# Phase 1's statistics two batches ahead, a difference moved from GpSimd to VectorE, and the first normalisation kept in memory for the second phase

## The chip, the cores and the metric

One core of a Trainium2 chip runs the kernel. The metric is the device time of one execution in microseconds. Five engines work side by side: TensorE (PE, with its weight loads PEld), VectorE (DVE), ScalarE (ACT), GpSimd (POOL) and SyncE (SP), which here issues nearly all DMAs.

## What is computed

The input x has 8 sequences of 512 tokens with 128 features. The block is a layer norm, a Mamba-like branch, a small branch of binary weights, and a sum. The reference, cut:

```python
xn = _layernorm(x)                              # (x - mean) / sqrt(var + eps)
# branch 1, on xn
normed = rmsnorm(xn, input_norm_w)
x_z, z = split(normed @ in_proj_W)              # 256 channels each
xc = silu(conv4(x_z) + conv_b)
dt = clip(softplus(xc @ dt_W + dt_b), 0.001, 0.1)
Bp, Cp = xc @ B_W, xc @ C_W                     # 64 states
h = exp(dt * A) * h + dt * B * xc               # 512 steps, per channel and state
y = einsum(h, C) * silu(z)
x1 = xn + y @ out_proj_W
n2 = rmsnorm(x1, ffn_norm_w)
a = x1 + (silu(n2 @ gate_W) * (n2 @ up_W)) @ down_W
# branch 2, on xn: weights of +1 and -1 from booleans
b = s2 * (relu2(s1 * (relu2(s0 * ([xn, -xn] @ k0)) @ k1)) @ k2)
out = x + a + b
```

## The kernel before

**Phase 1** works through eight batches (a sequence each), the tokens over the 128 partitions, four to a partition. `batches` lays it out in slots: in slot s an engine runs, in an order written in its own `slot(at)`, the stages of several batches, `at(stage, d)` for batch s + d. On VectorE the order is: `moments` of batch s+1 (mean and variance of each token), rests of b of batch s-2, `dt_bias` s-1, `normalize` s+1, `b_to_sbuf` s-1, `exp_to_p` s-1 (two steps of a compensated log(1 + e^v)), second rests s-2, `dt_and_u` s-1. GpSimd: `norms` s+1 (from the variance to the factor of layer norm, `nrm[:, 1]`, and to the product of both norms' factors, `nrm[:, 5]`, by seven small instructions), `first_rest` s-2, `log_err` s-1 (the difference `soft[:, 2] - soft[:, 1]`), `second_rest` s-2. `normalize` writes the input of the in-projection, with both norms in one factor, so layer norm's result alone is nowhere kept. TensorE: transposition of the normalised batch s, `dt_products` and `bc_products` s-1, `project` s (projection and convolution in one, L682). ScalarE: parts of u, copies, exp and log of the softplus (a table load each), and last `silus` of batch s, which `dt_products` of the next slot wait for. After slot 0 (`prepare_scan`) VectorE and GpSimd clear large tiles for the scan. SP stores each batch's dt, u and b to memory (`store`), and loads batches 4 to 7 of x into the places of batches 0 to 3 once those are normalised.

**The scan** has 512 steps in 16 bodies of 32. Each step k: GpSimd multiplies half of the state by its decay (L623, two instructions), VectorE multiplies the other half in PSUM (L1259) and adds the first half's input (L1270, two), ScalarE computes the decays of two steps in one exponential of 2048 columns (L1041), two steps ahead, and copies the PSUM half to SBUF (L1061), TensorE adds the inputs (L773, L780) and contracts the state with C (L828). SP loads the decays' exponents (L422, two DMAs of 512 KB for two steps, six places) and the chunks of inputs (12 DMAs for 16 steps, L201 to L218).

**The finish** of a group of 32 tokens per sequence rides in the scan: the function `finish(g, k)` of each engine gives what it does at step k after the end of group g's own body (negative: in that body, so -7 is step 25). It normalises x anew: `K_STATS` -7 and `K_MOMENTS` -6 on VectorE, `K_RSTD_SUM` -5 and `K_RSTD` -4 on GpSimd (a power), `K_SHIFT` -2 on VectorE, `K_XN` 0 on ScalarE (two activations); then at 2 TensorE transposes xn, and so on through the output projection (9), gate, up and down products and the binary branch to the result at 38. SP's `load_tokens(g)` loads x for group g in the middle of body g, two DMAs of 64 KB.

The three things that set the order are these programs in order on each engine, semaphores between them, and SP's queue. Bodies 3 to 14 are a hardware loop of three bodies (four rounds).

Of the kernel before, what the change touches and what calls it, by code (L numbers as in the profile page):

```python
# [5 lines left out]
F32 = mybir.dt.float32  # L6
BF16 = mybir.dt.bfloat16
U8 = mybir.dt.uint8
ALU = mybir.AluOpType
# [7 lines left out]
def mamba_and_binary_mlp_block(nc: bass.Bass, x, norm_w, ffn_w, in_w, conv_w, conv_b, dt_w, dt_b, b_w, c_w,  # L17
# [54 lines left out]
    dt_stage = nc.dram_tensor("dt_stage", (2, T // TS, Q, TS, E), F32, kind="Internal").ap()  # L72
    b_stage = nc.dram_tensor("b_stage", (NP, HQ, HQ, 2, NS, T, 2 * N), BF16, kind="Internal").ap()

    with ExitStack() as ctx:
# [84 lines left out]
        b_parts = c1.enter_context(nc.sbuf_tensor("b_parts", [P, 2, NP, NJ, 2 * N], BF16))  # L160
        w_in = c1.enter_context(nc.sbuf_tensor("w_in", [P, 2 * E], F32))
# [67 lines left out]
        def load_chunk(sp, t, cb, hq):  # L229
# [9 lines left out]
                 "b_zeroed cb_placed u_hi_ready b_hi_ready u_r1_ready b_r1_ready u_mid_ready b_mid_ready w1_step")  # L239
# [35 lines left out]
        def pb(name, shape, dt=F32):  # L275
# [18 lines left out]
        f_stats = pb("f_stats", [P, GT, 6])  # L294
        f_mv = pb("f_mv", [P, GT, 2])
        f_nrm = pb("f_nrm", [P, 5, GT])
# [13 lines left out]
        names = ("f_x_loaded f_stats_ready f_mv_ready f_rstd_ready f_shift_ready f_xn_ready f_xn_t_ready f_xn_feat_ready "  # L310
# [3 lines left out]
                 "f_result f_stored f_rstd_sum f_mean_square f_rrms_sum")  # L314
# [6 lines left out]
        K_STATS, K_MOMENTS, K_RSTD_SUM, K_RSTD, K_SHIFT, K_XN, K_XN_T, K_XN_FEAT = -7, -6, -5, -4, -2, 0, 2, 3  # L321
# [84 lines left out]
        with nc.Block() as block:  # L406
            @block.sync
            def _(sp):
# [17 lines left out]

                def store(q, bb):
# [5 lines left out]
                                 ).then_inc(S[f"dt_stored{bb}"], 16)  # L433
                    u_rows, b_planes = u_stage[q % HQ, q // HQ, bb], b_stage[:, q % HQ, q // HQ, bb]
# [97 lines left out]
            def _(pool):  # L532
# [32 lines left out]

                def log_err(q, bb):
                    n = q * 2 + bb

                    if n == B - 1:
                        return  # L570
# [839 lines left out]
```

## Time and profile before

| | |
|---|---|
| median of 3 runs | 1098.99 us (1097.10 to 1102.58) |
| the profiled execution | 1097.32 us |
| its span, first to last instruction | 1095.5 us |
| mean granted TensorE clock | 0.964 of full speed |
| busy: PE, DVE, ACT, POOL | 956.2, 915.3, 922.9, 847.7 us |
| DMA | 333.74 MB, mean 305 GB/s |
| first step of the scan | 177.6 us |
| starts of scan bodies 4, 5, 6 | 399.7, 453.7, 513.4 us |

The page gives, for one profiled execution, each engine's busy time, forty slices of the span, the chain that ended last, and the costliest groups of instructions. The trace behind it can be asked for timelines, waits and windows. A body that ends in the loop's jump (453.7 to 513.4) is about 5 us longer than others.

### The profile page before, as it was taken

To read this page: it belongs to the slowest core of one execution; us is meant where nothing else is said; L and a number is where in the kernel's file an instruction comes from. 1 tells how busy PE (TensorE), PEld (TensorE's weight loads), DVE (VectorE), ACT (ScalarE), POOL (GpSimd) and SP (SyncE) were. 2 spreads that over 40 slices of the span, in tenths; PEclk is the share of its full clock that TensorE was granted. 3 is DMA by queue.
4 is the path that set the end of the run, shared out by engine and by line. 5 is a ranking of instruction groups with operands and counts; after the bars stand their busy time and mean duration, and the time that the engine had idled before them with its cause. 6 is when DMAs were issued, how large, how long until landed. Compare 5 with 4: busy or idle time off the path is not lost.

```text
span 1095.5 us, 28254 instructions
## 1 busy us (share of the span) xinstructions
PE 956.2 (87%) x8006; PEld 424.3 (39%) x8006; DVE 915.3 (84%) x2035; ACT 922.9 (84%) x1125; POOL 847.7 (77%) x1216
## 2 busy tenths in 40 slices
PE   5988883568999999997999997999999899999898
PEld 3565541113434343433433332433333334343436
DVE  5677673998989999997999997898998899998992
ACT  1656776899989999997999997899997999999981
POOL 6555523888888888886888887898887798988880
PEclk9999986999999999998999999999999899999999
DMA  5245359999999999997899999898989799989940
GB/s 156 102 163 183 145 215 358 353 345 354 343 349 334 347 355 354 358 348 309 337 357 352 347 348 343 296 346 345 367 323 371 260 363 355 363 334 373 374 150 11
DMA packets 81004, 333.74 MB, mean 305 GB/s; under 512 B 15152, under 2 KB 35504, under 8 KB 45488
## 3 DMA queue, kind: packets, MB, share of 16 engines
q1 hardware_dynamic: 80688, 331.11, 81.8%
q8 instruction: 73, 1.20, 0.4%
q14 instruction: 115, 0.94, 0.2%
q10 hardware_dynamic: 128, 0.49, 0.1%
HBM read 306.38 MB, written 25.17 MB: 303 GB/s over the span
## 4 chain that ended last, share of the span: by engine, by line
PE 34%; DVE 26%; POOL 20%; issue 14%; ACT 3%; DMA 1%; DVEq 1%; ACTq 0%; SPq 0%; POOLq 0%
POOL decayed L623 14%; PE ps L828 11%; DVE ps L1259 8%; PE ps L773 7%; DVE state L1270 6%; PE ps L913 6%; PE ps L927 4%; DVE h L1367 2%; DVE soft L1185 2%; POOL soft L573 1%; PE ps L891 1%; PE ps L899 1%; PE ps L696 1%; ACT state L1061 1%; DVE gated L1332 1%
## 5 line engine op out<-in xcount | busy, mean ns | idle before, releaser
L623 POOL TENSOR_TENSOR decayed<-decay,state 128x256 f32<-128x256 f32 x1024 | 725.4, 733 | 152.5 <-DVE state L1270 103.9
L1041 ACT ACTIVATE decay<-decay,a_col 128x2048 f32<-128x2048 f32 x256 | 514.0, 2008 | 26.2 <-issue 17.9
L1270 DVE TENSOR_TENSOR state<-decayed,ps 128x256 f32<-128x256 f32 x1024 | 407.5, 418 | 58.8 <-POOL decayed L623 41.2
L1259 DVE TENSOR_TENSOR ps<-decay,ps 128x512 f32<-128x512 f32 x512 | 352.8, 689 | 41.1 <-ACT state L1061 16.0
L828 PE MATMUL ps<-state,c_cols 128*32 128x256 f32 x4096 | 336.8, 402 | 0.0
L1061 ACT COPY state<-ps 128x512 f32<-128x512 f32 x512 | 287.8, 587 | 54.7 <-issue 37.4
L773 PE MATMUL ps<-moving,b_rows 64*128 64x256 bf16 x1024 | 204.0, 280 | 89.9 <-DVE ps L1259 86.6
L780 PE MATMUL ps<-moving,b_rows 64*128 64x256 bf16 x1024 | 205.1, 282 | 13.0 <-DMA b_rows<-b_stage 13.0
L913 PE MATMUL ps<-h,w 128*128 128x256 f32 x512 | 176.8, 432 | 0.8 <-DVE h L1367 0.8
L773 PEld LDWEIGHTS ps<-moving,b_rows 64*128 64x128 bf16 x1024 | 58.4, 95 | 262.9 <-DVE ps L1259 163.7
L828 PEld LDWEIGHTS ps<-state,c_cols 128*32 128x32 f32 x4096 | 82.1, 110 | 112.3 <-issue 103.2
L913 PEld LDWEIGHTS ps<-h,w 128*128 128x128 f32 x512 | 80.3, 193 | 93.0 <-issue 90.0
L780 PEld LDWEIGHTS ps<-moving,b_rows 64*128 64x128 bf16 x1024 | 57.6, 95 | 13.3 <-issue 13.2
L682 PE MATMUL ps<-n_feat,w_tap 128*128 128x512 f32 x128 | 58.0, 607 | 1.0 <-ACT n_feat L947 1.0
L927 PE MATMUL ps<-w,h 128*128 128x128 f32 x256 | 44.7, 299 | 0.3 <-ACT h L1101 0.3
L878 PE MATMUL ps<-xn_feat,w 128*128 128x256 f32 x128 | 44.2, 430 | 0.3 <-DVE result L1376 0.2
L709 PE MATMUL ps<-w_dt,xc_feat 128*128 128x256 f32 x128 | 32.8, 410 | 12.3 <-ACT xc_feat L957 12.3
L927 PEld LDWEIGHTS ps<-w,h 128*128 128x128 f32 x256 | 33.5, 192 | 24.2 <-issue 23.4
L709 PEld LDWEIGHTS ps<-w_dt,xc_feat 128*128 128x128 f32 x128 | 30.5, 328 | 14.7 <-ACT xc_feat L957 14.1
L682 PEld LDWEIGHTS ps<-n_feat,w_tap 128*128 128x128 f32 x128 | 24.4, 196 | 29.2 <-issue 29.2
L1185 DVE TENSOR_TENSOR soft<-soft 128x1024 f32<-128x1024 f32 x8 | 20.8, 2602 | 16.3 <-POOL soft L573 16.3
L1145 DVE TENSOR_SCALAR normed<-x_tok,mean_var,nrm 128x128 f32<-128x128 f32 x32 | 19.9, 754 | 15.6 <-POOL nrm L564 15.6
(124 smaller groups left out, 813.2 us busy)
## 6 DMA issues: line engine op xcount, KB each, us to landing
decay<-dt_stage SPq DMA_DIRECT2D x512, 512.0 KB, 6.3
moving<-u_stage SPq DMA_DIRECT2D x63, 256.0 KB
u_stage<-u_parts SPq DMA_DIRECT2D x16, 512.0 KB, 2.8
b_rows<-b_stage SPq DMA_DIRECT2D x63, 128.0 KB
b_stage<-b_parts SPq DMA_DIRECT2D x16, 384.0 KB, 3.3
dt_stage<-dt_tok SPq DMA_DIRECT2D x8, 512.0 KB, 3.1
moving<-u_stage SPq DMA_DIRECT2D x126, 32.0 KB
x_tok<-in_L_attn_x_dram SPq DMA_DIRECT2D x4, 512.0 KB, 4.0
```

Source lines behind the costliest of these rows:

```text
L623: nc.gpsimd.tensor_tensor(decayed[:, p], decay[:, dec_slot(m, k), p, k % TS, :], state[:, (k - 1) % RING, p * E:(p + 1) * E], ALU.mult).th ...
L682: m = nc.tensor.matmul(ps[:, XC + h, :], w_tap[:, k, h * P:(h + 1) * P], n_feat[:, bass.ds(n, 1), k:k + T].rearrange("d o t -> d (o t)"), ...
L709: m = nc.tensor.matmul(ps[:, DTT + j // 2, (j % 2) * E:(j % 2 + 1) * E], xc_feat[:, bb, h, j:T:NJ], w_dt[:, h, :], start=(h == 0), stop=(h ...
L773: return nc.tensor.matmul(ps[:, acc_bank(m, k), p * E:(p + 1) * E], b_rows[rows(1), cb, p, kk, :], moving[rows(1), cb, kk, :], start=False ...
L780: return nc.tensor.matmul(ps[:, SELFP + k % 2, p * E:(p + 1) * E], b_rows[rows(0), cb, p, kk, :], moving[rows(0), cb, kk, :], start=True, ...
L828: m = nc.tensor.matmul(ps[q * 32:(q + 1) * 32, YP, 0:E], c_cols[:, cb, q, kk * 2 * TC:(kk + 1) * 2 * TC], state[:, k % RING, q * E:(q + 1) ...
L913: m = nc.tensor.matmul(ps[:, FB, c * GTOK:(c + 1) * GTOK], w1[:, n, f:f + P], h1[:, n, :], start=(n == 0), stop=(n == H1 // P - 1))
L927: m = nc.tensor.matmul(ps[:, FB, j * P:(j + 1) * P], terms[c][0][:, j * P:(j + 1) * P], terms[c][1], start=(c == 0), stop=(c == len(terms) ...
L1041: nc.scalar.activation(pair, pair, ACT.Exp, scale=a_col[:, 2:3]).then_inc(decay_ready, 1)
L1061: nc.scalar.copy(state[:, k % RING, SELF:QE], ps[:, acc_bank(m, k), :]).then_inc(acc_copied, 1)
L1259: nc.vector.tensor_tensor(ps[:, acc_bank(m, k), :].rearrange("p (q e) -> p q e", q=HQ), decay[:, dec_slot(m, k), HQ:Q, k % TS, :], ps[:, a ...
L1270: nc.vector.tensor_tensor(state[:, k % RING, p * E:(p + 1) * E], decayed[:, p], ps[:, SELFP + k % 2, p * E:(p + 1) * E], ALU.add).then_inc ...
```

## The change

It does four things. VectorE's `moments` move from the head of slot s for batch s+1 to near its end for batch s+2 (batch 0 before all slots). The difference that GpSimd's `log_err` made is made by VectorE in `exp_to_p`, as it was for the last batch before. A new stage `xn_tokens` on VectorE writes layer norm's result of each batch (x minus mean, times `nrm[:, 1]`) to a tile, from where SP stores it to `xn_stage` in memory, and SP's `load_tokens` loads it with x. The finish's own normalisation, the six steps `K_STATS` to `K_XN`, is gone.

```diff
+    xn_stage = nc.dram_tensor("xn_stage", (B, T, D), F32, kind="Internal").ap()
+        xnorm = c1.enter_context(nc.sbuf_tensor("xnorm", [P, NJ, D], F32))
 # SP
+                def store_xn(n):
+                    wait_all(sp, [(S["xnorm_ready"], n + 1)])
+                    sp.dma_start(xn_stage[n:n + 1].rearrange("o (p j) d -> p o (j d)", j=NJ),
+                                 xnorm[:].rearrange("p j d -> p (j d)").unsqueeze(1)).then_inc(S["xn_stored"], 16)
                 def store(q, bb):
                     ... # dt store
+                    if n + 2 < B:
+                        store_xn(n + 2)
+                store_xn(0)
+                store_xn(1)
                 for q in range(Q):
                         if n < B - XB and n % 2 == 0:
                             sp.wait_ge(S["normed_ready"], n + 2)
+                            sp.wait_ge(S["xnorm_ready"], n + 2)
                 sp.wait_ge(S["z_ready"], B)
+                sp.wait_ge(S["xn_stored"], 16 * B)
                 def load_tokens(g):
+                    for j in range(GT):
+                        sp.dma_start(xn[:, j, :], xn_stage[:, bass.ds(g * TG + j * TC, TC), :]
+                                     ).then_inc(G["f_xn_loaded"], 16)
 # GpSimd
                 def norms(q, bb):
                     after(pool, "moments_ready", n)
-                    after(pool, "normed_ready", n, back=1)
+                    after(pool, "xnorm_ready", n, back=1)
                 def slot(at):
                     at(norms, 1)
                     at(first_rest, -2)
-                    at(log_err, -1)
                     at(second_rest, -2)
                 def finish(g, k):
-                    if k == K_RSTD_SUM:
-                    ...
-                    if k == K_RSTD:
-                    ...
                     if k == K_BASE:
+                        pool.wait_ge(G["f_x_loaded"], (g + 1) * (16 * GT))
 # TensorE
                     if k == K_XN_T:
-                        after(pe, "f_xn_ready", g)
+                        pe.wait_ge(G["f_xn_loaded"], (g + 1) * (16 * GT))
 # ScalarE
-                    if k == K_XN:
-                    ...
 # VectorE
+                def xn_tokens(q, bb):
+                    n = q * 2 + bb
+                    after(dve, "xn_stored", n, per=16, back=1)
+                    for j in range(NJ):
+                        m = nc.vector.tensor_scalar(xnorm[:, j], token_tile(n, j), mean_var[:, bb, j, 0:1],
+                                                    nrm[:, 1, j:j + 1], ALU.subtract, ALU.mult)
+                    m.then_inc(S["xnorm_ready"], 1)
                 def exp_to_p(q, bb):
-                    if n == B - 1:
-                        after(dve, "p_ready", n)
-                        nc.vector.tensor_tensor(soft[:, 2], soft[:, 2], soft[:, 1], ALU.subtract
-                                                ).then_inc(S["log_err_ready"], 1)
+                    after(dve, "p_ready", n)
+                    nc.vector.tensor_tensor(soft[:, 2], soft[:, 2], soft[:, 1], ALU.subtract
+                                            ).then_inc(S["log_err_ready"], 1)
                 def slot(at):
-                    at(moments, 1)
                     at(first_rests, -2)
                     at(dt_bias, -1)
                     at(normalize, 1)
                     at(b_to_sbuf, -1)
                     at(exp_to_p, -1)
                     at(second_rests, -2)
+                    at(xn_tokens, 1)
+                    at(moments, 2)
                     at(dt_and_u, -1)
+                moments(0, 0)
                 batches(dve, slot, prepare_scan)
                 def finish(g, k):
-                    if k == K_STATS:
-                    ...
-                    if k == K_MOMENTS:
-                    ...
-                    if k == K_SHIFT:
-                    ...
```

## Rows read from the trace of the kernel before

**Rows 1.** Windows: span, busy PE, PEld, DVE, ACT, POOL; clock, DMA share, GB/s.
```profile
73.00:90.30 17.30, 14.78 (x54) 9.54 (x54) 12.55 (x23) 11.21 (x13) 9.91 (x10) 1.00 0.55 190
399.00:453.00 54.00, 50.02 (x474) 20.74 (x472) 49.72 (x116) 51.55 (x64) 47.56 (x70) 1.00 0.96 359
```
**Rows 2.** Timeline of PE, phase 1 (start, us, instruction, idle before): dt products.
```profile
38.66 4.12 PE L709 MATMUL ps<-w_dt,xc_feat 128*128 128x256 f32 x16 [1.19 <-ACT xc_feat L957]
...
54.27 4.11 PE L709 MATMUL ps<-w_dt,xc_feat 128*128 128x256 f32 x16 [0.50 <-ACT xc_feat L957]
...
88.88 4.11 PE L709 MATMUL ps<-w_dt,xc_feat 128*128 128x256 f32 x16 [2.23 <-ACT xc_feat L957]
...
139.45 4.11 PE L709 MATMUL ps<-w_dt,xc_feat 128*128 128x256 f32 x16 [1.26 <-ACT xc_feat L957]
```
**Rows 3.** Timeline of ACT in the slot from 73 us: the silu.
```profile
87.56 1.26 ACT L957 ACTIVATE xc_feat<-ps,cb_col 128x512 f32<-128x512 f32 x2
```
**Rows 4.** Timeline of POOL in the same slot: end of norms, and the difference.
```profile
80.15 0.20 POOL L564 TENSOR_TENSOR nrm<-nrm 128x4 f32<-128x4 f32 x1
...
85.02 2.46 POOL L573 TENSOR_TENSOR soft<-soft 128x1024 f32<-128x1024 f32 x1 [2.59 <-DVE soft L1174]
```
**Rows 5.** Timeline of DVE in the last batch: two subtractions of one form.
```profile
149.76 3.03 DVE L1178 TENSOR_TENSOR soft<-soft 128x1024 f32<-128x1024 f32 x1
...
153.04 1.21 DVE L1185 TENSOR_TENSOR soft<-soft 128x1024 f32<-128x1024 f32 x1
```
**Rows 6.** Timelines of DVE and of POOL at the start.
```profile
9.51 1.11 DVE L1145 TENSOR_SCALAR normed<-x_tok,mean_var,nrm 128x128 f32<-128x128 f32 x4
...
15.41 3.21 DVE L1145 TENSOR_SCALAR normed<-x_tok,mean_var,nrm 128x128 f32<-128x128 f32 x4 [3.59 <-POOL nrm L564]
...
28.49 1.19 DVE L1155 TENSOR_TENSOR soft<-ps,dtb_bc 128x1024 f32<-128x1024 f32 x1
...
18.96 3.51 POOL L608 MEMSET moving<- 128x4096 bf16 x1
```
**Rows 7.** Groups of instructions by line: busy us, mean ns of one; the finish's normalisation.
```profile
L1083 ACT ACTIVATE xn<-x_in,f_nrm 128x128 f32<-128x128 f32 x32 | 14.0, 490 | 0.0
...
L635 POOL TENSOR_TENSOR f_nrm<-f_nrm,mhalf 128x2 f32<-128x2 f32 x16 | 11.2, 697 | 0.0
...
L1320 DVE SCALAR_TENSOR_TENSOR f_nrm<-f_mv,f_nrm 128x2 f32<-128x2 f32 x16 | 7.3, 457 | 0.0
...
L1315 DVE BATCH_NORM_AGGREGATE f_mv<-f_stats 128x2 f32<-128x6 f32 x32 | 3.9, 164 | 0.0
```
**Rows 8.** Timeline of DVE in the scan: steps 25, 29 and 3.
```profile
443.40 0.48 DVE L1309 BATCH_NORM_STATS2 f_stats<-x_in 128x6 f32<-128x128 f32 x2
...
449.52 0.42 DVE L1270 TENSOR_TENSOR state<-decayed,ps 128x256 f32<-128x256 f32 x1 [0.43 <-POOL decayed L623]
...
458.93 0.69 DVE L1259 TENSOR_TENSOR ps<-decay,ps 128x512 f32<-128x512 f32 x1 [0.43 <-ACT state L1061]
```
**Rows 9.** Timeline of PE in the scan: the first matmul of steps 26, 27, 28, 30, 2.
```profile
444.54 0.28 PE L773 MATMUL ps<-moving,b_rows 64*128 64x256 bf16 x1 [0.42 <-DVE ps L1259]
...
446.28 0.28 PE L773 MATMUL ps<-moving,b_rows 64*128 64x256 bf16 x1 [0.15 <-DVE ps L1259]
...
447.80 0.28 PE L773 MATMUL ps<-moving,b_rows 64*128 64x256 bf16 x1
...
451.20 0.28 PE L773 MATMUL ps<-moving,b_rows 64*128 64x256 bf16 x1 [0.29 <-DVE ps L1259]
...
457.90 0.28 PE L773 MATMUL ps<-moving,b_rows 64*128 64x256 bf16 x1 [0.74 <-DVE ps L1259]
```
**Rows 10.** Timeline of ACT in the scan: the exponential for step 0.
```profile
448.90 2.00 ACT L1041 ACTIVATE decay<-decay,a_col 128x2048 f32<-128x2048 f32 x1 [0.43 <-DMA decay<-dt_stage]
```
**Rows 11.** Waits of SP from 349 to 507 us: total, times, longest.
```profile
SPq L422 <- DVE state L1270: 8.3, 6, 2.3
```
**Rows 12.** Timeline of SP in the scan: the two loads of x.
```profile
476.43 1.51 SPq L480 DMA_DIRECT2D x_in<-in_L_attn_x_dram  x2
```

More of the change, by code:

```diff
@@ L564, in norms @@
                     nc.gpsimd.tensor_tensor(nrm[:, 5], nrm[:, 4], nrm[:, 1], ALU.mult).then_inc(S["rms_ready"], 1)
-                def log_err(q, bb):
-                    n = q * 2 + bb
-                    if n == B - 1:
-                        return
-                    after(pool, "p_ready", n)
-                    after(pool, "dt0_ready", n, back=1)
-                    nc.gpsimd.tensor_tensor(soft[:, 2], soft[:, 2], soft[:, 1], ALU.subtract
-                                            ).then_inc(S["log_err_ready"], 1)
                 def first_rest(q, bb):
@@ L627, in finish @@
                 def finish(g, k):
-                    if k == K_RSTD_SUM:
-                        after(pool, "f_mv_ready", g)
-                        after(pool, "f_xn_ready", g, back=1)
-                        nc.gpsimd.tensor_tensor(f_nrm[:, 0], f_mv[:, :, 1], eps_t[:, 0:GT], ALU.add
-                                                ).then_inc(G["f_rstd_sum"], 1)
-                    if k == K_RSTD:
-                        after(pool, "f_rstd_sum", g)
-                        nc.gpsimd.tensor_tensor(f_nrm[:, 1], f_nrm[:, 0], mhalf[:, 0:GT], ALU.pow
-                                                ).then_inc(G["f_rstd_ready"], 1)
                     if k == K_RRMS_SUM:
@@ L1077, in finish @@
                 def finish(g, k):
-                    if k == K_XN:
-                        after(act, "f_shift_ready", g)
-                        act.wait_ge(G["f_x_loaded"], (g + 1) * (16 * GT))
-                        after(act, "f_x1_ready", g, back=1)
-                        for j in range(GT):
-                            m = nc.scalar.activation(xn[:, j], x_in[:, j], ACT.Identity, bias=f_nrm[:, 4, j:j + 1],
-                                                     scale=f_nrm[:, 1, j:j + 1])
-                        m.then_inc(G["f_xn_ready"], 1)
                     if k == K_N2:
@@ L1089, in finish @@
                         for j in range(GT):
-                            m = nc.scalar.activation(n2[:, j], x1[:, j], ACT.Copy, scale=f_nrm[:, 3, j:j + 1])
+                            m = nc.scalar.activation(n2[:, j], x1[:, j], ACT.Copy, scale=f_nrm[:, 1, j:j + 1])
                         m.then_inc(G["f_n2_ready"], 1)
@@ L1304, in finish @@
                 def finish(g, k):
-                    if k == K_STATS:
-                        dve.wait_ge(G["f_x_loaded"], (g + 1) * (16 * GT))
-                        after(dve, "f_rstd_ready", g, back=1)
-                        for j in range(GT):
-                            m = nc.vector.bn_stats(f_stats[:, j], x_in[:, j])
-                        m.then_inc(G["f_stats_ready"], 1)
-                    if k == K_MOMENTS:
-                        after(dve, "f_stats_ready", g)
-                        nc.vector.memset(wait_mark[:], 0.0)
-                        for j in range(GT):
-                            m = nc.vector.bn_aggr(f_mv[:, j], f_stats[:, j])
-                        m.then_inc(G["f_mv_ready"], 1)
-                    if k == K_SHIFT:
-                        after(dve, "f_rstd_ready", g)
-                        after(dve, "f_xn_ready", g, back=1)
-                        nc.vector.scalar_tensor_tensor(f_nrm[:, 4], f_mv[:, :, 0], -1.0, f_nrm[:, 1], ALU.mult, ALU.mult
-                                                       ).then_inc(G["f_shift_ready"], 1)
                     if k == K_XN_FEAT:
```

20 lines of the change are left out of this document (8 added, 12 removed).

## The prediction

> **What bounds the kernel now.** I read the stages first, by the windows of busy time [rows 1]. Phase 1 (eight batches through projection, convolution, softplus) is 170 us, the scan of 512 steps with its folded-in finish some 880 us, a tail of 30 us follows. In a batch slot of phase 1 (73.0 to 90.3) no engine is full: TensorE 14.78 of 17.30 us, VectorE 12.55, ScalarE 11.21, GpSimd 9.91. So a chain sets the slot. In a group of 32 scan steps (399 to 453) four engines and the DMA are nearly full together: TensorE 50.0 of 54, VectorE 49.7, ScalarE 51.6, GpSimd 47.6, DMA share 0.96 at 359 GB/s. There an edit is worth only what the next engine lets through.
>
> Next the chain of waits of a slot, followed in the engines' timelines. TensorE starts a batch's dt products at 38.66, 54.27 and 88.88 [rows 2]: one slot of 15.6 us at the start, then two of 17.3 each. Before 88.88 TensorE idled 2.23 us for ScalarE's silu. That silu ran at 87.56 [rows 3], because the logarithm before it in ScalarE's order came late, and that one waited for VectorE, which waited for the norms: moments, then 3.7 us of small GpSimd instructions ending at 80.35 [rows 4], then u_rest (2.1 us) on GpSimd beside the normalisation. GpSimd then takes the softplus difference at 85.02, 2.46 us [rows 4], and second_rest behind it; VectorE's next subtraction needs the difference and runs beside second_rest, which stretches it to some 3 us as in [rows 5].
>
> **Phase 1, part by part.**
> Moments one batch earlier: nothing is removed; the moments stand in the slot before, so GpSimd's norms run while VectorE ends the previous slot. The normalisation then finds its scale ready, and the chain moments - norms - normalisation leaves the slot.
> The difference on VectorE: GpSimd's 2.46 us leave the chain [rows 4]; VectorE takes it on. Undisturbed such a subtraction is 1.21 us, beside GpSimd's second_rest it was 3.03 us in the last batch, where VectorE does it already [rows 5]. Those are the two ends.
> Normalised x kept (xn_tokens): four instructions of VectorE per batch, by the same form undisturbed 1.11 us, beside a GpSimd instruction 3.21 us [rows 6]. One store of 256 KB per batch, on SP's queue behind the dt store, ahead of the u and b stores: one issue, about the 0.75 us that half of the pair in [rows 12] took. SP's next store waits for u_mid, several us away, so I put it at nothing; if the cover is gone, it is 0.75 us a slot on no chain that VectorE sees. VectorE's wait for the store of the batch before (xn_stored) holds up moments and the dt steps queued behind it; it was issued a slot earlier, so nothing again in steady state.
> The sum by engine: VectorE's 12.55 us [rows 1] include one subtraction already stretched to 3; plus 1.21 plus 1.11 is 14.9 us; TensorE 14.78 plus the silu that it cannot pass, 0.7 us (half of the pair of 1.26) [rows 3], is 15.5 us. So TensorE sets the slot at about 15.6, as it did from 38.66 to 54.27 [rows 2]. From 38.66 to 139.45 are six slots [rows 2], 100.8 us; six of 15.6 are 93.6: **7.2 us gained**. After 139.45 the last batch goes as before: its difference was already VectorE's.
>
> The start pays something back. Moments(1) now stand behind xn_tokens(0): +1.1 us. The first two batches' xn_tokens come before VectorE's own memsets, which the dt bias of batch 0 (at 28.49 [rows 6]) queues behind. xn_tokens(1) begins at about 20 and meets GpSimd's memset (3.51 us at 18.96 [rows 6], then some 1.3 us later) as the normalisation did (3.21 us at 15.41): it ends at about 24 instead of the 18.6 at which VectorE was free. With moments(2) the dt bias of batch 0 starts 5.8 us later, at 34.3. The way from there to TensorE's 38.66 was 10.2 us, and 2.5 us of it was the wait for the norms that now is gone: 42.0, so 3.4 us late. If the four instructions slip in before the memset, only 0.6 us late. The first is nearer to the row, the second to the order in which the queues arrive: I take 2. **Phase 1: 5.2 us gained**, bounds 8 gained (the late start costs nothing, slots a little under 15.6) and 3 lost (rival b).
>
> What a page says here is the opposite of the change's intent. The rows show 3.03 us against 1.21 for the same form [rows 5]. The Trainium skill (SBUF — State Buffer, section "SBUF: two separate sides") says that an instruction of VectorE with two SBUF inputs and one of GpSimd that reads SBUF hold their shared port pair exclusively, so the later one waits whole. The trace agrees. By that rule the moved difference costs VectorE up to 3 us in every slot; it stands below as a rival.
>
> **The scan, part by part.** Removed per group [rows 7, 8]: VectorE two statistics, two aggregates with a memset, one shift. Instructions overlap their neighbours (the pair of statistics lasts 0.48 us, the next instruction starts after 0.40), so they weigh about 0.4, 0.15 and 0.4, together **0.95 us**. GpSimd: the small add and the power, 0.20 and 0.70. ScalarE: two xn activations, paired 0.77 to 0.87. TensorE loses nothing. Where they stand: the statistics in steps 25 and 26, GpSimd's power at step 28, the shift at step 30, ScalarE's at step 0 of the next group.
> Is it on the path? At step 29 VectorE waits 0.43 us for GpSimd, which is running the power; at step 3 it waits 0.43 us for ScalarE's state copy, which stands behind the xn activations [rows 8]. TensorE waits 0.42 us for VectorE behind the statistics and 0.74 at step 2 [rows 9]. So all removed work is on the path at its place, 0.95 + 0.43 + 0.43 = 1.8 us if nothing else came next. Something does. Between steps 24 and 31 TensorE runs back to back at 1.52 us a step except for waits of 0.42, 0.15 and 0.29 [rows 9]: 0.86 us is all that this stretch can give. And ScalarE's exponential for step 0 waited 0.43 us for its decay transfer [rows 10]: this transfer leaves SP behind twelve chunk loads, at a time that the removed work doesn't move, so what VectorE gains there it partly waits for at step 31. Going through the steps in order with these spacings leaves 0.8 us a group where no transfer is late and 0.4 where it lands 1 us later. I take **0.7 us x 16 groups = 11.2 us, bounds 0.2 and 1.2 (3 and 19 us)**.
>
> What it adds: two loads of xn per group on SP, behind the two of x_in, which took 1.51 us to issue [rows 12]; behind them stand two pairs of decay loads, then the next chunk. In the three groups from 349 to 507 SP waited 8.3 us for VectorE before decay loads, 2.8 a group, the longest 2.3 [rows 11]: 1.5 us more fits into these waits. Without that cover a late decay pair would cost up to 1.5 us a group. TensorE's transposition now waits for that load, a quarter of a group early; nothing there. GpSimd's base now waits for x_in, landed long before. The bytes: 131 KB on some 359 x 54 = 19.4 MB a group [rows 1], at the same rate 0.36 us of DMA time, on a DMA with 4% to spare: that is why I take 0.7 and not 0.8.
> The Trainium skill (DMA: Bandwidth & Descriptors, section "Specifications") puts HBM's limit per core at about 358 GB/s. The row's 359 agrees with it being close. By it a group of 19.5 MB could not go below an estimated 54.5 us, and the scan would gain nothing: rival (a).
>
> The tail loses 0.87 us of ScalarE's work, but TensorE gets to xn's transposition later than that anyway: 0.
>
> **The sum.** Profiled execution 1097.32 us (span 1095.5 and 1.8 around it). 1097.3 - 5.2 - 11.2 = 1080.9. The median shown is 1098.99, 1.7 above the profiled one: **1083**.
>
> **Rivals.**
> (a) The DMA becomes the bound of the scan. For: share 0.96, ScalarE already waits for decays [rows 1, 10]. Against: such waits are rare, and a saturated DMA would make them the rule. The scan gives 0 to 3 us, phase 1 its 5: 1092.
> (b) The shared port takes back the slot. For: 3.03 us [rows 5], 3.21 us [rows 6]. VectorE's 14.9 us plus one more block of 1.8 is 16.7 a slot, six of them 100.2; with a start 3.4 us late phase 1 loses 3. Against: second_rest starts only after ScalarE's cast, when the difference may be done. 1099 - 11 + 3 = 1091.
> (c) Slower. SP has no room where the loads are put: the decay pairs behind them leave 1.5 us late, and ScalarE, and with it all, waits that long in each group. It decides from the point where the extra 1.5 us exceed SP's wait between x_in and the next chunk. 16 x 1.5 = 24 lost, the scan's 11 and phase 1's 5 gained: 1107. Against: SP's waits [rows 11].
> (d) All goes through: 1.2 us a group, 19, and 8 in phase 1: 1072.
> That the kept xn isn't what the scan needs isn't a rival: it is the same value, stored and loaded.
>
> **Chances.** Forecast (1076 to 1089) 0.57, (a) 0.14, (b) 0.12, (c) 0.07, (d) 0.10. The range takes in (a), (b) and most of (d): 1072 to 1094. Half a per cent, 5.5 us, is about what a measurement of this kernel tells from no change. Faster by more: forecast, (d), (b) and half of (a), 0.84; within 0.10; slower 0.06.
>
> **What would show it.** The dt products of TensorE 15.5 to 15.7 us apart, with an idle time before them under 1 us; VectorE's difference at 1.2 us (right) or 3 (rival b). The dt bias of batch 0 at 31 to 34. Groups of scan steps near 53.3 us where the one from 399.7 to 453.7 took 54.0; no VectorE wait at steps 29 and 3; a longer wait of ScalarE for decays means (a); SP without waits around x_in means (c). I am wrong if the slots stay at 17, if the scan's groups don't shrink, or if both give twice what I sum.

## The result, and the profile after

The changed kernel took 1085.07 us (median of 4 runs, 1083.14 to 1089.68) beside 1098.05 us of the kernel before (4 runs): a ratio of 0.9896, 95% interval 0.9865 to 0.9928. The forecast was 1083 in a range of 1072 to 1094. The profiled execution took 1084.61 us with a span of 1082.5, where before had 1095.5; the sum of the prediction had given 1080.9 for it.

The page of the changed kernel, busy time of each engine (us, share of the span, instructions), the granted clock in 40 slices and the DMA total:

```profile
PE 952.5 (88%) x8006; PEld 423.1 (39%) x8006; DVE 917.3 (85%) x1978; ACT 909.1 (84%) x1093; POOL 826.1 (76%) x1177
...
PEclk9899996689999999998999999999999999999999
...
DMA packets 86506, 337.91 MB, mean 312 GB/s; under 512 B 15537, under 2 KB 39985, under 8 KB 50993
```

The first and the last step of the scan divide the gain between the stages. The view by line of VectorE's multiplication in PSUM, one for each step, gives its count, its durations (shortest, median, longest, in ns) and its first and last start in us:

```profile
L1255 DVE TENSOR_TENSOR ps<-decay,ps x512: 681/689/697, 176.5 to 1053.0; 128x512 f32<-128x512 f32 x171
```

The same line in the kernel before:

```profile
L1259 DVE TENSOR_TENSOR ps<-decay,ps x512: 672/689/697, 177.6 to 1066.5; 128x512 f32<-128x512 f32 x171
```

So phase 1 ends 1.1 us earlier, the scan takes 876.5 us where it took 888.9 (12.4 less), and the tail is some 0.5 us longer.

**Phase 1.** The windows of the changed kernel (as [rows 1]):

```profile
42.00:60.00 18.00, 14.81 (x45) 9.84 (x46) 12.78 (x27) 11.80 (x15) 9.09 (x9) 0.78 0.20 74
60.00:76.00 16.00, 15.36 (x54) 9.73 (x54) 14.30 (x29) 11.77 (x14) 9.04 (x9) 1.00 0.52 189
...
62.47:77.91 15.44, 14.80 (x52) 9.53 (x52) 13.74 (x28) 11.21 (x13) 9.04 (x9) 1.00 0.54 196
...
399.00:453.00 54.00, 50.89 (x486) 21.18 (x482) 49.56 (x112) 51.28 (x64) 47.84 (x70) 1.00 0.96 369
```

The timeline of TensorE with the dt products (L704), answering [rows 2]:

```profile
39.56 1.04 PE L665 MATMUL ps<-ident,normed 128*128 128x128 f32 x4 [2.69 <-DVE normed L1132]
44.89 6.25 PE L704 MATMUL ps<-w_dt,xc_feat 128*128 128x256 f32 x16 [4.28 <-ACT xc_feat L952]
...
62.47 4.11 PE L704 MATMUL ps<-w_dt,xc_feat 128*128 128x256 f32 x16 [0.34 <-ACT xc_feat L952]
77.91 4.12 PE L704 MATMUL ps<-w_dt,xc_feat 128*128 128x256 f32 x16 [0.34 <-ACT xc_feat L952]
...
139.69 4.11 PE L704 MATMUL ps<-w_dt,xc_feat 128*128 128x256 f32 x16 [0.78 <-ACT xc_feat L952]
```

Two things are to be seen. From 62.47 on the slots are 15.44 us and TensorE waits only 0.34 us in front of the dt product, where it had waited 2.23. But batch 1 comes at 44.89 instead of 38.66, 6.2 us late, and the slot after it takes 17.6. There the granted clock is 0.78 as a mean, so a part of the stretch ran at the lower of the two levels, 1.2 GHz in place of 2.4, after TensorE had stood still for 2.69 and 4.28 us; the same 16 products took 6.25 us in place of 4.1. The slots win back what the start lost: at 139.69 the kernel is where the one before was (139.45).

The cause stands in VectorE's timeline at the start (answering [rows 6]), and beside it GpSimd's:

```profile
10.61 1.11 DVE L1140 TENSOR_SCALAR xnorm<-x_tok,mean_var,nrm 128x128 f32<-128x128 f32 x4
...
19.64 7.79 DVE L1140 TENSOR_SCALAR xnorm<-x_tok,mean_var,nrm 128x128 f32<-128x128 f32 x4
...
37.33 1.16 DVE L1150 TENSOR_TENSOR soft<-ps,dtb_bc 128x1024 f32<-128x1024 f32 x1
```
```profile
20.08 3.51 POOL L611 MEMSET moving<- 128x4096 bf16 x1
23.52 3.51 POOL L612 MEMSET b_rows<- 128x4096 bf16 x1
```

The four instructions that keep the normalised x of batch 1 took 7.79 us where they need 1.11: both of GpSimd's clearings went by before they were through. All that is queued behind them on VectorE is late, the dt bias of batch 0 by 8.8 us against [rows 6].

The difference on VectorE with the kept xn and the next subtraction behind it, and the GpSimd instruction beside the difference (answering [rows 4, 5]):

```profile
57.34 3.03 DVE L1172 TENSOR_TENSOR soft<-soft 128x1024 f32<-128x1024 f32 x1
...
60.63 1.11 DVE L1140 TENSOR_SCALAR xnorm<-x_tok,mean_var,nrm 128x128 f32<-128x128 f32 x4
...
62.85 1.19 DVE L1179 TENSOR_TENSOR soft<-soft 128x1024 f32<-128x1024 f32 x1
```
```profile
56.86 2.42 POOL L595 TENSOR_TENSOR u_parts<-u_rest,u_parts 128x1024 bf16<-128x1024 f32 x1 [5.00 <-ACT u_parts L1003]
```

From here on the difference is held for 3.03 us, not 1.21, in every slot. But in the kernel before the subtraction behind it (L1185, now L1179) was the one that was held there:

```profile
87.58 3.07 DVE L1185 TENSOR_TENSOR soft<-soft 128x1024 f32<-128x1024 f32 x1 [2.29 <-POOL soft L573]
```

The hold has moved from one subtraction to the other and was not added: VectorE is busy 13.74 us in a slot (62.47 to 77.91) where it was 12.55, about the 1.1 us of the kept xn more, and the slot's end is TensorE's (14.80 of 15.44 us, with a wait of 0.34 for the silu).

**The scan.** VectorE and TensorE where [rows 8, 9] stand for before:

```profile
448.51 0.42 DVE L1266 TENSOR_TENSOR state<-decayed,ps 128x256 f32<-128x256 f32 x1 [0.17 <-POOL decayed L626]
...
457.41 0.68 DVE L1255 TENSOR_TENSOR ps<-decay,ps 128x512 f32<-128x512 f32 x1
```
```profile
454.93 0.28 PE L768 MATMUL ps<-moving,b_rows 64*128 64x256 bf16 x1 [0.74 <-DVE ps L1255]
```

VectorE's waits of 0.43 us for the power and for ScalarE's copy have gone or shrunk to 0.17; TensorE's wait of 0.74 us at step 2 has stayed. SP's timeline (the four loads) and its waits from 349 to 507 us, as [rows 11, 12]:

```profile
473.10 1.51 SPq L492 DMA_DIRECT2D x_in<-in_L_attn_x_dram  x2
474.72 1.31 SPq L495 DMA_DIRECT2D xn<-xn_stage  x2
```
```profile
SPq L422 <- DVE state L1266: 4.3, 4, 1.8
```

The wait before decay loads fell from 8.3 to 4.3 us in three groups: the new issues took 1.3 us a group out of it. Over the whole run ScalarE waited 12.6 us for decay loads, 12 times, where it had been 8.1.

### The profile page after: what moved, and what is told of

It reads as the page before. It is cut to its first block, busy times and chain, and to the rows that moved or that the text cites. A ratio compares the mean times of both kernels' runs of the same rounds, so it can differ in the third digit from the quotient of the medians.

```text
span 1082.5 us, 28111 instructions
## 1 busy us (share of the span) xinstructions
PE 952.5 (88%) x8006; PEld 423.1 (39%) x8006; DVE 917.3 (85%) x1978; ACT 909.1 (84%) x1093; POOL 826.1 (76%) x1177
## 4 chain that ended last, share of the span: by engine, by line
PE 39%; DVE 26%; POOL 13%; issue 13%; ACT 4%; SPq 2%; DMA 2%; DVEq 1%; ACTq 0%; POOLq 0%
POOL decayed L626 12%; PE ps L823 10%; DVE ps L1255 10%; DVE state L1266 7%; PE ps L768 7%; PE ps L908 5%; PE ps L922 5%; PE ps L677 4%; PE ps L704 3%; DVE h L1346 2%; ACT state L1056 2%; PE ps L886 2%; PE ps L894 1%; PE ps L716 1%; DMA decay<-dt_stage 1%
## 5 line engine op out<-in xcount | busy, mean ns | idle before, releaser
L775 PE MATMUL ps<-moving,b_rows 64*128 64x256 bf16 x1024 | 205.2, 282 | 11.9 <-DMA b_rows<-b_stage 11.9
L908 PE MATMUL ps<-h,w 128*128 128x256 f32 x512 | 173.7, 425 | 0.8 <-DVE h L1346 0.8
L704 PE MATMUL ps<-w_dt,xc_feat 128*128 128x256 f32 x128 | 35.0, 431 | 7.2 <-ACT xc_feat L952 7.2
L704 PEld LDWEIGHTS ps<-w_dt,xc_feat 128*128 128x128 f32 x128 | 31.7, 329 | 10.8 <-ACT xc_feat L952 9.2
L595 POOL TENSOR_TENSOR u_parts<-u_rest,u_parts 128x1024 bf16<-128x1024 f32 x7 | 17.0, 2427 | 22.9 <-ACT u_parts L1003 22.9
L567 POOL TENSOR_TENSOR nrm<-mean_var,eps_t 128x4 f32<-128x4 f32 x8 | 6.0, 755 | 36.5 <-DVE mean_var L1116 36.5
```

Source lines behind the costliest of these rows:

```text
L704: m = nc.tensor.matmul(ps[:, DTT + j // 2, (j % 2) * E:(j % 2 + 1) * E], xc_feat[:, bb, h, j:T:NJ], w_dt[:, h, :], start=(h == 0), stop=(h ...
L775: return nc.tensor.matmul(ps[:, SELFP + k % 2, p * E:(p + 1) * E], b_rows[rows(0), cb, p, kk, :], moving[rows(0), cb, kk, :], start=True, ...
L908: m = nc.tensor.matmul(ps[:, FB, c * GTOK:(c + 1) * GTOK], w1[:, n, f:f + P], h1[:, n, :], start=(n == 0), stop=(n == H1 // P - 1))
```

## The experiments

Each diff is against the changed kernel unless said otherwise. For comparison across kernels I use the first and last start of this multiplication, as above.

**1. GpSimd's clearings late.** Both clearings stand behind all batches on GpSimd's queue.
```
-                    nc.gpsimd.memset(moving[:, 0], 0.0)
-                    nc.gpsimd.memset(b_rows[:, 0], 0.0).then_inc(rows_zeroed, 1)
                 batches(pool, slot, prepare_scan)
+                nc.gpsimd.memset(moving[:, 0], 0.0)
+                nc.gpsimd.memset(b_rows[:, 0], 0.0).then_inc(rows_zeroed, 1)
```


> The changed kernel, with GpSimd's two large clearings (moving, b_rows, 3.5 us each) moved from the start to the end of phase 1. Theory 1 (the start is lost to GpSimd's clearings, which hold up VectorE's xn_tokens of batch 1 for 7.8 us): xn_tokens of batch 1 takes 1.1 us, the dt bias of batch 0 starts at 31 instead of 37.3, TensorE's dt products of batch 1 at 38 to 39 instead of 44.9 and at full clock (4.1 us, not 6.25); the whole about 8 us faster, 1077. Theory 2 (TensorE's late second batch is due to VectorE's own clearings, 8.8 us, or to the weights): at most 1 to 2 us faster, 1084.

Measured: 1082.44 us (before on that chip 1098.69), ratio 0.9859 (0.9832 to 0.9885). The dt products of batches 1 and 7 stood at 38.84 and 131.52: the start's loss was gone, as theory 1 had it, and batch 7 came 8.2 us earlier. But the kernel missed theory 1's 1077. The scan's first step came at 172.4, only 4.1 us earlier. VectorE's timeline in the last batch, and GpSimd's, show the other 4:

```profile
146.35 4.86 DVE L1183 TENSOR_SCALAR dt_tok<-soft 128x1024 f32<-128x1024 f32 x1
```
```profile
143.70 3.51 POOL L612 MEMSET moving<- 128x4096 bf16 x1
147.15 3.51 POOL L613 MEMSET b_rows<- 128x4096 bf16 x1
```

The clip, 0.69 us elsewhere, now stood beside the clearings. The collision had been moved, not removed.

**2. VectorE's own clearings late too** (its c_cols and b_rows behind the batches).


> As the run before, and VectorE's clearing of c_cols and b_rows (3.5 and 1.8 us) moved to the end of phase 1 as well, where it has 7 us idle before the scan. Theory 1: the dt bias of batch 0 starts at 26.5, as soon as TensorE has its products; the dt products of batch 1 at 37.7, when their convolution is done; 1 us less than the run before, 1076. Theory 2: slots of 15.45 us are TensorE's own bound, so nothing more comes after the second batch. If the clearings at the end delay the scan's first loads, the scan starts later instead, and the whole is as the run before.

Measured: 1084.1 us, ratio 0.9857 (0.983 to 0.9884), first step at 172.2. The dt bias of batch 0 came at 27.39 instead of experiment 1's 31.27, but the dt product of batch 1 only at 38.62 instead of 38.84, and the 1 us that theory 1 had put on it did not come: VectorE's own clearings cost the start nothing more. With the scan's code unchanged, this profile's scan took 884.5 us, 8 more than in 1: that is how far one profiled scan can lie from another.

**3. Clearings after the last u.** As 1, with a wait for the last batch's u ahead of them.
```
                 batches(pool, slot, prepare_scan)
+                pool.wait_ge(S["u_ready"], B)
+                nc.gpsimd.memset(moving[:, 0], 0.0)
```


> The changed kernel, with GpSimd's two clearings (moving and b_rows, 3.51 us each) moved behind a wait for the last batch's VectorE step that makes u, so that they stand beside nothing of VectorE's in phase 1. In the first of these experiments they stood beside VectorE's clip of the last dt, which took 4.86 us in place of 0.69. Theory A (the clearings hold back whatever VectorE does beside them, and that alone ate half of what the start had given): the last batch's clip takes about 0.7 us, the scan's first step starts at about 168.3 (172.4 less the 4.1 us), and the kernel takes about 1078. Rival (the end of phase 1 is set by something else, so the 4 us don't come through): first step at 172 and 1082. Rival (the clearings are now the last thing that the first step waits for, 7 us after u): first step at 173 to 175, 1083 to 1085.

Measured: 1079.71 us (1073.26 to 1080.65), ratio 0.9822 (0.9782 to 0.9861), first step at 167.6. The clip (VectorE) was back at its own duration, with the clearing (GpSimd) behind it:

```profile
145.50 0.69 DVE L1184 TENSOR_SCALAR dt_tok<-soft 128x1024 f32<-128x1024 f32 x1
```
```profile
147.51 3.51 POOL L613 MEMSET moving<- 128x4096 bf16 x1 [4.60 <-DVE u_tok L1189]
```

So these two instructions cost the changed kernel's profiled execution 8.9 us of phase 1 where they stood (176.5 less 167.6). Theory A holds.

**4. Phase 1's changes with the old finish.** The kernel before with xn_tokens, its stores, the statistics two ahead and the difference on VectorE; the finish normalises as before and loads no xn.


> The changed kernel with the finish's own normalisation (statistics, power, shift, xn) as in the kernel before, and without the loads of xn; phase 1 as changed, its xn store kept. Theory 1 (nearly all of the gain is the scan's, phase 1 gives 1 us): 1097, within 0.3% of the kernel before. Theory 2 (the extra loads cost the scan something that the removed work hides): 1099 or more gained back elsewhere; then groups of scan steps shorter than before's. Groups of 54.0 to 54.4 us away from the loop's jumps support theory 1.

Measured: 1098.18 us over 10 runs, ratio 1.0003 (0.9984 to 1.0022), scan from 176.5 to 1066.0. Theory 1 holds: with the start's loss in it, all of phase 1 is worth nothing.

**5. The new finish with phase 1's order of before.** The changed kernel with statistics one batch ahead and the difference on GpSimd.


> The finish of the changed kernel (xn stored in phase 1 and loaded in the scan), with phase 1's two other edits undone: statistics one batch ahead, difference on GpSimd. The kernel with phase 1 changed and the old finish took the time of the kernel before (ratio 1.0003). Theory A (the two halves add up; phase 1's is worth nothing since its start gives back what its slots win): 1085 to 1087, first step at 177.6, slots of 17.3 us. Theory B (the start's loss comes from the third set of statistics alone, and the slots' gain is what it costs to the us): dt product of batch 1 at about 38.7 as before. Rival (the halves depend on each other: the stores of xn in phase 1, or the longer slots, cost here): 1090 or more.

Measured: 1098.25 us over 10 runs, ratio 1.0014 (0.9991 to 1.0037). A and B fell (the slots were neither 17.3 nor was batch 1 back at 38.7: its dt product came at 43.86); the rival stood: the halves depend on each other, and neither gains anything alone. By line:

```profile
L1267 DVE TENSOR_TENSOR ps<-decay,ps x512: 681/689/697, 185.3 to 1063.0; 128x512 f32<-128x512 f32 x171
```

The scan (877.7 us) is as short as in the changed kernel, but it begins at 185.3, 7.7 us later than in the kernel before. That is the price of keeping xn in the old order. 5.2 us of it stand at the start (batch 1's dt product at 43.86 instead of 38.66; in this profile the xn instructions of batch 1 met one of GpSimd's clearings, 4.19 us), and six slots add 3.7 (batch 7 at 148.38 instead of 139.45); the last batch gives 1.2 back. What a slot loses is seen in the timelines of VectorE, GpSimd and TensorE:

```profile
92.13 4.98 DVE L1152 TENSOR_SCALAR xnorm<-x_tok,mean_var,nrm 128x128 f32<-128x128 f32 x4
```
```profile
91.96 2.47 POOL L588 TENSOR_TENSOR soft<-soft 128x1024 f32<-128x1024 f32 x1 [2.59 <-DVE soft L1181]
94.39 2.13 POOL L606 TENSOR_TENSOR u_parts<-u_rest,u_parts 128x1024 bf16<-128x1024 f32 x1
```
```profile
95.83 4.11 PE L716 MATMUL ps<-w_dt,xc_feat 128*128 128x256 f32 x16 [1.51 <-ACT xc_feat L964]
...
113.82 5.63 PE L716 MATMUL ps<-w_dt,xc_feat 128*128 128x256 f32 x16 [2.27 <-ACT xc_feat L964]
```

The xn instructions are held by GpSimd's difference and then by second_rest, 4.98 us for 1.11, and the slots are 18.0 us from 77.85 on, longer than the 17.3 of [rows 2]. In the slot from 113.82 the dt products also took 5.63 us in place of 4.11: the granted clock was 0.89 as a mean from 108 to 124.

**6. Only the difference back on GpSimd.**


> The changed kernel with the correction's difference back on GpSimd; the statistics stay two batches ahead. The slots of phase 1 (from dt product to dt product) are 15.45 us in the changed kernel and end on TensorE's products there; with both edits undone they were 17.98 us. Theory A (the statistics two ahead take GpSimd's and VectorE's waits out of the slot, and it alone makes the slots 15.45, since TensorE ends them): slots 15.4 to 15.6, first step at 176 to 177, 1085. Theory B (both are needed: with the difference on GpSimd VectorE waits 2.4 us for it in each slot and spends as much less beside it): slots 16.2 to 17.3, first step 5 to 11 us later than in the changed kernel, 1090 to 1096. Rival (the difference on GpSimd is the better place, since VectorE's 3.03 us beside it fall away): slots 15.4 and the late slots' VectorE share lower, no time gained.

Measured: 1088.98 us (5 runs), ratio 0.9911 (0.9881 to 0.9941), slots of 16.1 us (94.64, 110.80, 126.96), first step at 179.3. It lies between A and B. VectorE's xn again took 4.98 us beside the two GpSimd instructions:

```profile
106.04 4.98 DVE L1152 TENSOR_SCALAR xnorm<-x_tok,mean_var,nrm 128x128 f32<-128x128 f32 x4
```

With 5 and the changed kernel this gives each edit's worth by the slot: 17.3 us before; 18.0 with xn kept alone (+0.7); 16.1 with the statistics two ahead as well (-1.8); 15.45 with the difference on VectorE as well (-0.7). In the changed kernel the xn instructions take 1.11 us again (60.63). The first steps (177.6, 185.3, 179.3, 176.5) can't be subtracted in this way, since the starts differ: 5 met one of GpSimd's clearings, 6 and the changed kernel both (7.79 us), and the first xn of 6 began 0.9 us later than the changed kernel's.

**7. Each load of xn issued twice.** The added one goes into a tile that nobody reads; it stands ahead of the kept one, and TensorE waits for both.
```
+                        sp.dma_start(xn_copy[:, j, :], xn_stage[:, bass.ds(g * TG + j * TC, TC), :]
+                                     ).then_inc(G["f_xn_loaded"], 16)
```


> The changed kernel with each xn load made twice (the second into a spare tile): two more DMAs of 64 KB per group on SP. Theory 1 (SP's queue still has room: it waits 5 us a group): 0 to 3 us slower, 1085 to 1088. Theory 2 (rival c: SP's order puts decay loads late by what is put ahead of them): 1.5 us per group, 24 us slower, 1109, and ScalarE's waits for decays grow from 0.8 to over 2 us a group.

Measured: 1098.27 us over 10 runs, ratio 0.9998 (0.998 to 1.0015); scan from 176.3 to 1066.3, 890.0 us. Two more loads cost all that the scan had gained, 13 us. ScalarE's waits for decay loads over the whole run, the changed kernel first (total, times, longest):

```profile
ACT decay L1036 <- DMA decay<-dt_stage: 12.6, 12, 3.8
```
```profile
ACT decay L1039 <- DMA decay<-dt_stage: 31.0, 33, 3.1
```

They grew by 18.4 us, to 1.9 a group, close to what theory 2 had said (over 2), and SP's own waits before decay loads fell from 20.7 to 11.9 us. By the pages the median decay load took 6.7 us from issue to landing against 6.5 in the changed kernel (and 6.7 in 3, where nothing of this was lost), so the loads came late mainly because they were issued late, not because they took longer. The changed kernel stands close to the point from which rival (c) decides; the time lost is half of theory 2's.

**8. Two tiny loads more.** As 7, but with one row of 512 B each.


> The changed kernel and two more loads of 512 B a group on SP's queue, into a tile that nobody reads: SP's issue without the bytes. The kernel with each of the two xn loads issued twice was 13 us slower than the changed one. Theory A (what costs there is SP's time, which the issue of a DMA takes whatever it moves): if a small DMA takes SP as long as one of 128 rows, 1098; if its issue is shorter in proportion to its rows, near 1085. The issue rows tell which of the two it is, and the groups' periods must follow the issue time. Theory B (the bytes, 128 KB more a group, cost): 1085 to 1087, with issues as long as those of the large loads.

Measured: 1086.11 us (6 runs), ratio 0.9908 (0.9881 to 0.9934). SP's timeline:

```profile
470.68 1.31 SPq L496 DMA_DIRECT2D xn<-xn_stage  x2
472.09 0.69 SPq L499 DMA_DIRECT2D xn_copy<-xn_stage  x2
```

The pair took SP 0.69 us, half of a pair of 128 rows. The scan was 878.7 us: 2.2 more than the changed kernel's, inside the spread of such scans. ScalarE waited 13.3 us for decay loads, hardly more than the 12.6. So half of the issue time costs about nothing and the whole of it, with its bytes, 13 us. That fits a cover that is used up, but this run alone doesn't separate SP's time from the 131 KB; the landing times of 7 speak for SP's time.

The start of this kernel is that of the changed one, and yet the xn instructions met one clearing only (VectorE, then GpSimd):

```profile
19.66 4.19 DVE L1145 TENSOR_SCALAR xnorm<-x_tok,mean_var,nrm 128x128 f32<-128x128 f32 x4
```
```profile
20.10 3.60 POOL L616 MEMSET moving<- 128x4096 bf16 x1
23.65 3.66 POOL L617 MEMSET b_rows<- 128x4096 bf16 x1
```

VectorE got in between the two, and the first step came at 172.2 instead of 176.5. Who gets in at that seam is worth 4.3 us, and VectorE's and GpSimd's programs up to there are the same in this kernel and the changed one. Of the nine profiles with xn kept and the clearings in their old place, six met both (7.8 us: the changed kernel, 4, 6, 7, 11 and 12) and three met one (4.19 us: 5, 8 and 10). Which of the two an execution without a profile had isn't known. The forecast's worst case for the start (end at 24, dt bias at 34.3, dt product at 42.0) is nearly what came here: 23.85, 33.74 and 41.31.

**9. Two loads of 1 KB rows.** As 3, with x copied beside the kept xn in phase 1 (memory to memory, 8 DMAs), so that each group needs two loads in place of four.
```
-                        sp.dma_start(x_in[:, j, :], x[:, bass.ds(g * TG + j * TC, TC), :]
+                        sp.dma_start(xx[:, j].rearrange("p o d -> p (o d)"),
+                                     xn_stage[:, bass.ds(g * TG + j * TC, TC), :, :].rearrange("b t o d -> b t (o d)")
```


> The same as the kernel with the clearings behind the last u, and in memory x and xn of a token lie side by side (x is copied from memory to memory in phase 1, 8 more DMAs), so that SP issues two loads of 1 KB rows a group instead of four of 512 B. Theory A (SP's order is nearly full in the changed kernel, and its two more issues, 0.75 us each, cost some tenths of a us in some groups): SP's waits in the groups grow by 1.5 us, the decay loads land earlier before their exponentials, and the kernel is 1 to 4 us faster than the other with late clearings, 1074 to 1077. Rival (SP has room, the issues cost nothing): no difference, 1078. Rival (the bytes of the loads delay the decay loads, not their issues): no difference either, since the bytes are the same. Rival (the copies in phase 1 cost VectorE or SP time there): the first step later than in the other kernel, and slower by that.

Measured: 1078.02 us (1076.54 to 1081.94), ratio 0.9831 (0.9796 to 0.9866). The scan took 878.7 us against 881.4 in 3, but 876.5 in the changed kernel. The two kernels with the clearings behind the last u, 3 and 9, are the fastest here, and not distinguishable from each other, so theory A is not confirmed.

**10. VectorE's share put back as dead work:** statistics at k=-7, aggregates at -6, shift at -2.


> The changed kernel with VectorE's share of the old first normalisation put back as dead work on the same steps: the statistics (k=-7), the aggregates (k=-6) and the shift (k=-2) of the group's x, into tiles that nobody reads. GpSimd's and ScalarE's shares stay out, and the loads stay as changed. The finish gave the scan 11 to 12 us in all (from first to last step 876.5 us against 888.9). Theory A (VectorE's instructions carry most of it, since VectorE or GpSimd ends each step): first to last step 883 to 887, 1091 to 1095. Rival (GpSimd's two small instructions carry it, since GpSimd's decayed ends most steps): 877 to 880, 1085 to 1088.

Measured: 1105.8 us over 10 runs, ratio 1.0084 (1.006 to 1.0109), scan 900.7 us (172.8 to 1073.5; its start met one clearing). The scan grew by 24.2 us, twice what the removal had brought, and neither theory's range holds. VectorE's timeline shows where:

```profile
508.39 0.69 DVE L1259 TENSOR_TENSOR ps<-decay,ps 128x512 f32<-128x512 f32 x1 [5.26 <-issue]
513.57 0.75 DVE L1270 TENSOR_TENSOR state<-decayed,ps 128x256 f32<-128x256 f32 x2 [4.48 <-issue]
```

Most of the scan is a loop of three bodies, and at each of its three turns every kernel here stands for some 5 us ("issue": nothing that the profile shows). Here VectorE stands a second time, 4.48 us, one instruction later. The six groups on either side of the turns took 356.0 us together, against 338.6 to 341.0 in the six profiles with the changed finish (below). The six groups between, away from the turns, averaged 53.7 us.

**11. GpSimd's share put back** (one small addition at k=-5, one small power at k=-4, on constants).


> The changed kernel with GpSimd's share put back as dead work: one small addition at k=-5 and one small power at k=-4 a group, on constants. Theory A (a part of the gain is GpSimd's own, since four multiplications fill its step): 2 to 6 us of the 12 come back, first to last step 879 to 883, 1087 to 1091. Rival (VectorE carries all of it): 876 to 878, 1084 to 1087. Rival (GpSimd carries all of it): 887 or more, 1095.

Measured: 1088.91 us over 10 runs, ratio 0.9921 (0.9897 to 0.9946), scan 880.0 us. This is in theory A's range, but also inside the spread of scans without the dead work.

**12. ScalarE's share put back** (two 128x128 activations at k=0 into a spare tile).


> The changed kernel with ScalarE's share put back as dead work: the two 128x128 activations on x_in at k=0 into a spare tile, in place of nothing. Theory A (ScalarE has room at that step, since what it waits for there is the decay load): no more than 2 us of the 12 come back, 876 to 879 from first to last step, 1084 to 1088. Rival (ScalarE's exponentials follow each other without a pause, and what is put between them delays the chain): each group 0.6 us longer, 885, 1094.

Measured: 1090.68 us over 9 runs, ratio 0.9925 (0.9906 to 0.9943), scan 882.5 us: more than theory A allowed, less than the rival.

11 and 12 can't be told from each other, and hardly from the changed kernel (0.9865 to 0.9928). The group times away from the turns say the same: 53.3 and 54.0 us on average, where six profiles with the changed finish (the changed kernel, 1, 2, 3, 5 and 6) gave 53.2 to 53.9, and the two with the old finish 54.3 (before) and 54.0 (4). So the scan's gain is there as a whole, but no engine's share of it was resolved. Experiment 10 doesn't settle VectorE's share either: some 16 of its 24 us are the second stops at the turns, which the kernel before, with nearly the same instructions, doesn't have.

## Why the prediction was right, and where it was not

**The slots: right.** 15.6 us forecast with TensorE as their end, 15.44 measured, with a wait of 0.34 us ahead of the dt product. The reason was right too, with experiments 5 and 6 added to it: of the 2.5 us between slots of 18.0 and 15.45 the statistics carry 1.8 and the difference 0.7. I had said that both take an instruction out of one chain. What the runs show is another part: moving the difference away from GpSimd also frees the kept xn from being held 4.98 us. One term was too large: I had put VectorE at 14.9 us a slot, the difference on top of a subtraction already held, and it was 13.74, because the hold moved to the difference and left that subtraction at 1.19.

**The start: the term that was mis-sized.** It was "it ends at about 24", for xn_tokens(1), and from it a dt bias at 34.3 and 2 us lost. I had counted one clearing in its way. It met both and ended at 27.43; the dt bias came at 37.33. From there to the dt product of batch 1 it was 7.6 us, just the 10.2 less 2.5 of the working, so only the hold was mis-sized. Experiment 8's profile, which met one clearing, kept to the forecast's worst case. What I had not foreseen at all is the second part, 2.1 us in the next slot at the lower clock (17.6 against 15.45). Loss: 6.2 and 2.1, where my worst bound was 3.4. Phase 1 therefore gained 1.1 us and not 5.2: at batch 7 it was 0.2 us behind, and 1.3 came from the last batch, for which I had put nothing. Experiment 3 shows what the slots had won once the clearings are out of the way: the first step at 167.6, 10.0 us ahead of the kernel before.

What the row shows at 19.64 is a VectorE instruction with one tensor input, held by a GpSimd instruction that only writes. The Trainium skill (SBUF — State Buffer, section "SBUF: two separate sides") says of the shared port pair, for a VectorE instruction in a 2-port perf mode or with two SBUF inputs (the latter only against a GpSimd instruction that reads SBUF), and for GpSimd's, that the one that starts first "gets the pair for the whole instruction; the other fully blocks". The trace agrees with 7.79 us across two clearings of 3.51, if these instructions run in such a mode, which no row says, and adds that the wait need not end with the first of them.

**The scan: right within its spread.** 11.2 us forecast, 12.4 in the profiled pair. The six profiles with the changed finish took 876.4 to 884.5 us (mean 879.2), the two with the old one 888.9 and 889.5: a gain of 10.0 on average. In the six groups away from the loop's turns it is some 0.6 us a group (54.1 less 53.5), against my 0.7. That all removed steps were on the path, each at its place, is not confirmed: putting one engine's share back moved those groups by no more than the spread.

**SP "at nothing": right, but with little left.** The two loads did fit into SP's waits (8.3 to 4.3 us in three groups). Experiment 7 shows the price once they don't fit: 13 us for the next pair, where rival (c) had put 24, with ScalarE's waits for decay loads up from 12.6 to 31.0 us.

**The rivals.** (a) The DMA as a bound: no. The window from 399 to 453 moved 369 GB/s in the changed kernel and 359 before, at a share of 0.96 in both. By the rate of 358 GB/s that the Trainium skill (DMA: Bandwidth & Descriptors, section "Specifications") puts as HBM's limit per core, the groups could not have shrunk; they did, so here the measurement decides. (b) The shared port: its mechanism was there in each slot, 3.03 us, but not as one block more: the subtraction held before (3.07 us) took 1.19, and TensorE had the slot. The port decided at the start instead, and in experiments 5 and 6. (d): nothing that I gave it came about, but experiments 3 and 9 come down to 1078 to 1080 by taking the start's loss away.

The time was thus met with a phase 1 that brought 4.1 us less than said and a scan that brought 1.2 more (or 1.2 less, by the mean). That the total still lay near the forecast says little for the part on phase 1: the slots' own length bears out the slots, and a start that took back nearly all of it still fitted into a range of 22 us, which is luck as far as the time goes.

## What to carry to other kernels

A change that adds VectorE work to a stage must be laid beside what GpSimd does at that moment, the one-off clearings at the start included: here two of them, 7 us in all, took back 8.9 of the 10.0 us that phase 1 had won. Move such an instruction behind a wait for the last VectorE result that it could hold up, not only to the end of its own queue; the end of the queue was worth 4.1 us, the wait 8.9. Two edits that each bring nothing alone (experiments 4 and 5) can be worth 13 us together, so the price of an addition is to be read in the order in which it will run.

## What the runs showed of the hardware that I had not expected

- The same program start ended two ways: four VectorE instructions of 1.11 us took 7.79 us in one kernel's profile and 4.19 in another's, depending on whether they got in between two GpSimd instructions that follow each other at once. It is worth 4.3 us of 1085, and of nine profiles six had the first and three the second.
- TensorE's granted clock was 0.78 in the stretch from 42 to 60 us, with TensorE idle for 2.69 and 4.28 us ahead of its instructions at 39.56 and 44.89; without these waits, in experiment 3, it stayed at 1.00 and the slot was 15.45 us.
- Six small VectorE instructions and their waits in a loop body brought a second stop of 4.07 to 4.48 us at the turns of the loop. Its cause is not shown by any row.
- An issue of a DMA took SP 0.35 us with one row of 512 B and 0.65 with 128 rows.
